# One ring of three PSUM banks for turned probabilities and jobs, in place of one bank and two

## What is computed

```python
qkv = (x @ w_qkv).reshape(b, s, NUM_HEADS + 2 * NUM_KV, HEAD_DIM)
...
logits = jnp.einsum('bkpsd,bktd->bkpst', q, k) * scale
attn = jax.nn.softmax(logits.astype(jnp.float32), axis=-1)
combined = jnp.einsum('bkpst,bktd->bkpsd', attn, v.astype(jnp.float32)).astype(v.dtype)
...
return combined @ w_out
```

## Time and profile before

| | us |
|---|---|
| median of 3 runs | 3746.49 |
| lowest, highest | 3746.47, 3748.72 |
| the profiled execution | 3749.1 |
| its span, first to last instruction | 3747.4 |
| TensorE busy | 3391.4 |
| VectorE busy | 2742.9 |
| ScalarE busy | 2060.3 |
| GpSimd busy | 1140.2 |

### The profile page before, as it was taken

How to read it: one execution, slowest core, us unless ns; L and a number is a source line. 1 busy time by engine, 2 the same in 40 slices (tenths; PEclk the granted TensorE clock), 3 DMA queues, 4 the chain that set the end, 5 groups by cost and what they waited for, 6 DMA issues and landing times.

```text
span 3747.4 us, 52800 instructions
## 1 busy us (share of the span) xinstructions
PE 3391.4 (90%) x19398; PEld 2853.6 (76%) x19398; DVE 2742.9 (73%) x5009; ACT 2060.3 (55%) x3891; POOL 1140.2 (30%) x1507
## 2 busy tenths in 40 slices
PE   2788888879999999999999999999999999999993
PEld 1677777767878888788887887878887888788872
DVE  4787897757786777776777677776777767776764
ACT  2567766745545555555555555555555555556541
POOL 2577877842212212122121221212212121122103
PEclk9999999989999999999999999999999999999996
DMA  2000001110000000000000001000000010000000
GB/s 75 20 24 24 25 28 35 43 32 12 15 14 27 21 13 12 12 21 26 12 13 13 23 19 40 12 12 24 26 14 13 18 29 25 12 23 22 25 6 28
DMA packets 81103, 83.27 MB, mean 22 GB/s; under 512 B 8272, under 2 KB 76496, under 8 KB 80720
## 3 DMA queue, kind: packets, MB, share of 16 engines
q1 hardware_dynamic: 80848, 79.89, 7.2%
HBM read 74.62 MB, written 5.24 MB: 21 GB/s over the span
## 4 chain that ended last, share of the span: by engine, by line
PE 64%; DVE 8%; ACT 5%; issue 1%; DMA 0%; POOL 0%; DVEq 0%; SPq 0%; ACTq 0%; POOLq 0%
PE at_ps_t L1717 12%; PE at_ps_job L35 6%; PE at_ps_job L37 6%; PE at_ps_job L36 6%; PE at_ps_o L37 5%; PE at_ps_o L35 5%; PE at_ps_o L36 5%; PE at_ps_s L37 5%; PE at_ps_s L35 5%; PE at_ps_s L36 5%; DVE at_probT_lo L1598 2%; ACT at_probT_hi L1544 1%; ACT x_resident L1587 1%; PE at_ps_job L852 1%; DVE ch_r L742 1%
## 5 line engine op out<-in xcount | busy, mean ns | idle before, releaser
L1544 ACT ACTIVATE at_probT_hi<-at_ps_t 128x512 fp32r<-128x512 f32 x1024 | 611.2, 597 | 1152.4 <-PE at_ps_t L1717 1152.2
L1598 DVE TENSOR_TENSOR at_probT_lo<-at_ps_t,at_probT_hi 128x512 fp32r<-128x512 f32 x1024 | 705.1, 689 | 377.1 <-ACT at_probT_hi L1544 365.4
L1717 PE MATMUL at_ps_t<-ident,x_resident 128*128 128x128 f32 x4096 | 625.6, 275 | 103.1 <-DVE at_probT_lo L1598 92.3
L1717 PEld LDWEIGHTS at_ps_t<-ident,x_resident 128*128 128x128 f32 x4096 | 481.0, 140 | 254.9 <-DVE at_probT_lo L1598 113.8
L1652 DVE TENSOR_REDUCE at_neg_max<-at_ps_s 128x1 f32<-128x1024 f32 x512 | 623.0, 1217 | 10.9 <-PE at_ps_s L37 2.4
L1587 ACT ACTIVATE x_resident<-at_ps_s,at_neg_max 128x1024 f32<-128x1024 f32 x512 | 569.4, 1112 | 12.9 <-DVE at_neg_max L1652 9.8
L1527 POOL TENSOR_TENSOR at_w_hi<-at_w_raw,ch_cols 128x256 fp32r<-128x256 f32 x192 | 117.7, 613 | 1196.5 <-PE at_ps_job L37 1175.4
L35 PE MATMUL at_ps_o<-at_probT_hi,at_v_lo 128*128 128x512 f32 x1024 | 445.8, 435 | 2.4 <-DVE at_oT_lo L1628 2.4
L35 PE MATMUL at_ps_s<-at_k_hi,at_q_lo 128*128 128x512 f32 x1024 | 447.3, 437 | 0.0
L37 PE MATMUL at_ps_s<-at_k_lo,at_q_hi 128*128 128x512 f32 x1024 | 405.3, 396 | 0.0
L37 PE MATMUL at_ps_o<-at_probT_lo,at_v_hi 128*128 128x512 f32 x1024 | 404.0, 395 | 0.0
(11 more groups left out here) (275 smaller groups left out, 7781.5 us busy)
## 6 DMA issues: line engine op xcount, KB each, us to landing
at_w_raw<-attn_w SPq DMA_DIRECT2D x256, 128.0 KB, 2.3
at_w_raw<-mlp_w SPq DMA_DIRECT2D x112, 128.0 KB, 2.3
li_wq_raw<-lin_q_w SPq DMA_DIRECT2D x64, 128.5 KB, 2.1
li_wo_raw<-lin_out_w SPq DMA_DIRECT2D x32, 256.0 KB, 3.0
x_resident<-x SPq DMA_DIRECT2D x4, 1024.0 KB, 10.8
out<-x_resident SPq DMA_DIRECT2D x4, 1024.0 KB, 5.0
li_raw<-mlp_w SPq DMA_DIRECT2D x16, 128.0 KB, 2.4
ch_r<-lin_kv_w SPq DMA_DIRECT2D x1, 1024.0 KB, 6.7
```

The lines of the kernel that those rows point to most:

```text
L1544: nc.scalar.activation(ph[:, i // TC, 4 * half:4 * half + 4, (i % TC) * P:(i % TC + 1) * P], ps_t[:], ACT.Copy).then_inc(s_ph, 1)
L1598: nc.vector.tensor_tensor(pl[at], ps_t[:], ph[at].bitcast(F32), ALU.subtract).then_inc(s_pl, 1)
L1717: last = nc.tensor.transpose(ps_t[:, j, :], prob[:, i % 2, kt * P:(kt + 1) * P], sh.ident[:])
```

## The change

The two sets of banks become one ring of three. `Plan` numbers the two turns of a slot and its jobs together, in TensorE's order but with both turns first (`claim`), and before a turn or job is issued `wait_emptied` waits for whoever reads out the claim three back. `at_ps_t` is gone; turns are written to and read from `at_ps_job`, which has three banks. Both turns' waits for the turn before them go. The order of instructions on every engine is the same as before; what changes is the bank that an instruction names and the semaphore count it waits for. The linear attention phase uses the same classes with two banks and no turns, as before.

```diff
-    def __init__(self, begin, end, rows, chain, tail):
+    def __init__(self, begin, end, rows, chain, tail, banks, turns=lambda t: ()):
...
         for t in range(self.begin, self.end):
+            for number in turns(t):
+                self.claim["TURNED", number] = len(self.taker)
+                self.taker.append(("turn", number + 1))
             for kind, v, part in rows(t):
                 self.count(kind, v, part)
...
         self.place[key] = len(self.place)
+        self.claim[key] = len(self.taker)
...
-        self.taker.append((kind in ACT_TAKES, counts[key]))
+        self.taker.append(("act" if kind in ACT_TAKES else "dve", counts[key]))
...
     def bank(self, kind, v, part):
-        return self.ps_job[self.plan.place[kind, v, part] % 2]
+        return self.ps_job[self.plan.claim[kind, v, part] % self.plan.banks]
+
+    def turned_bank(self, number):
+        return self.ps_job[self.plan.claim["TURNED", number] % self.plan.banks].rearrange("p (j t) -> p j t", j=4)
...
+def wait_emptied(pe, c, n):
+
+
+    if n >= c.plan.banks:
+        by, count = c.plan.taker[n - c.plan.banks]
+        pe.wait_ge({"act": c.took, "dve": c.taken, "turn": c.turned_low}[by], count)
+
+
 def claim(pe, c, kind, v, part):
-
-
-    n = c.plan.place[kind, v, part]
-    if n >= 2:
-        by_act, count = c.plan.taker[n - 2]
-        pe.wait_ge(c.took if by_act else c.taken, count)
-    return c.ps_job[n % 2]
+    wait_emptied(pe, c, c.plan.claim[kind, v, part])
+    return c.bank(kind, v, part)
...
+def turned_tile(t):
+
+
+    u, slot = divmod(t, TB)
+    back, i = (u - 1, slot + TB - 2) if slot < 2 else (u, slot - 2)
+    return (back, i) if 0 <= back < UNITS else None
+
+
+def turns_at(t):
+    if turned_tile(t):
+        u, i = turned_tile(t)
+        yield 2 * TB * u + 2 * i
+        yield 2 * TB * u + 2 * i + 1
...
         ps_s = [ctx.enter_context(nc.psum_tensor(f"at_ps_s{i}", [P, S], F32)) for i in range(2)]
-        ps_t = ctx.enter_context(nc.psum_tensor("at_ps_t", [P, 4, P], F32))
         ps_o = ctx.enter_context(nc.psum_tensor("at_ps_o", [P, CH], F32))
-        ps_job = [ctx.enter_context(nc.psum_tensor(f"at_ps_job{i}", [P, CH], F32)) for i in range(2)]
+        ps_job = [ctx.enter_context(nc.psum_tensor(f"at_ps_job{i}", [P, CH], F32)) for i in range(3)]
...
             def turn(u, i, half):
+                number = 2 * TB * u + 2 * i + half
+                wait_emptied(pe, c, plan.claim["TURNED", number])
+                turned = c.turned_bank(number)
                 for j in range(4):
                     kt = 4 * half + j
-                    last = nc.tensor.transpose(ps_t[:, j, :], prob[:, i % 2, kt * P:(kt + 1) * P], sh.ident[:])
+                    last = nc.tensor.transpose(turned[:, j, :], prob[:, i % 2, kt * P:(kt + 1) * P], sh.ident[:])
                 last.then_inc(s_pT, 1)
...
                 if turned:
+                    back, i = turned
                     pe.wait_ge(s_exp, TB * back + i + 1)
-                    if 2 * TB * back + 2 * i:
-                        pe.wait_ge(s_pl, 2 * TB * back + 2 * i)
                     turn(back, i, 0)
...
                 values_part(u, slot, 0)
                 if turned:
-                    pe.wait_ge(s_pl, 2 * TB * back + 2 * i + 1)
                     turn(back, i, 1)
```

More of the change, by code:

```diff
@@ L352 @@
 class Plan:
-    def __init__(self, begin, end, rows, chain, tail):
-        self.rows = rows
+    def __init__(self, begin, end, rows, chain, tail, banks, turns=lambda t: ()):
+        self.rows, self.banks = rows, banks
         self.at, self.first, self.last = {}, {}, {}
@@ L378, in __init__ @@
                 self.no[kb] = i if kinds != ("X",) else kb[1]
-        self.place, self.high, self.by_dve, self.by_act, self.taker = {}, {}, {}, {}, []
+        self.place, self.claim, self.high, self.by_dve, self.by_act, self.taker = {}, {}, {}, {}, {}, []
         for t in range(self.begin, self.end):
+            for number in turns(t):
+                self.claim["TURNED", number] = len(self.taker)
+                self.taker.append(("turn", number + 1))
             for kind, v, part in rows(t):
@@ L474, in sem @@
             return sh.sem(f"{tag}_{name}")
-        self.plan, self.ps_job, self.tile = plan, ps_job, tile
+        self.plan, self.ps_job, self.tile, self.turned_low = plan, ps_job, tile, None
         self.ln = Ln(sh, tag)
@@ L921, in linear_attention_phase @@
     plan = Plan(BEGIN, END + LAG + 2, lambda t: rows.get(t, []),
-                [("QA", 2, 0), ("QA", 3, 0), ("QB", 0, LOOP + LAG + 2), ("FA", 0, 0), ("X", 0, 3 * LOOP + 1)], [])
+                [("QA", 2, 0), ("QA", 3, 0), ("QB", 0, LOOP + LAG + 2), ("FA", 0, 0), ("X", 0, 3 * LOOP + 1)], [], 2)
     made, high, by_dve = plan.made, plan.high, plan.by_dve
@@ L1387, in attention_phase @@
                 [("QB", 1, 4), ("FA", 1, 0), ("X", 1, 0), ("QB", 2, 0), ("FA", 2, 0), ("X", 2, 0), ("FB", 0, TB * H + TB),
-                 ("QB", 3, 0), ("FA", 3, 0), ("X", 3, 0), ("FB", 1, 2 * TB * H + TB), ("FB", 2, 3 * TB * H + TB)], [("FB", 3)])
+                 ("QB", 3, 0), ("FA", 3, 0), ("X", 3, 0), ("FB", 1, 2 * TB * H + TB), ("FB", 2, 3 * TB * H + TB)], [("FB", 3)], 3, turns_at)
     made, high, by_dve, by_act = plan.made, plan.high, plan.by_dve, plan.by_act
@@ L1433, in attention_phase @@
         c.first_x = 1
+        c.turned_low = s_pl
         block = ctx.enter_context(nc.Block())
@@ L1544, in probT_high @@
                 nc.scalar.activation(ph[:, i // TC, 4 * half:4 * half + 4, (i % TC) * P:(i % TC + 1) * P],
-                                     ps_t[:], ACT.Copy).then_inc(s_ph, 1)
+                                     c.turned_bank(2 * TB * u + 2 * i + half), ACT.Copy).then_inc(s_ph, 1)
             def job_high(u, slot, late=False):
@@ L1573, in _ @@
                 has_last, has_own = u >= 1, u < UNITS
-                back, i = (u - 1, slot + TB - 2) if slot < 2 else (u, slot - 2)
-                turned = has_last if slot < 2 else has_own
+                turned = turned_tile(t)
                 if turned:
+                    back, i = turned
                     probT_high(back, i, 0)
@@ L1597, in probT_low @@
                 at = (slice(None), i // TC, slice(4 * half, 4 * half + 4), slice((i % TC) * P, (i % TC + 1) * P))
-                nc.vector.tensor_tensor(pl[at], ps_t[:], ph[at].bitcast(F32), ALU.subtract).then_inc(s_pl, 1)
+                nc.vector.tensor_tensor(pl[at], c.turned_bank(2 * TB * u + 2 * i + half), ph[at].bitcast(F32),
+                                        ALU.subtract).then_inc(s_pl, 1)
             def job_low(u, slot, late=False):
```

## The result

The changed kernel takes 3615.5 us (median of 4 runs, 3613.0 to 3617.2), the one before 3747.6 beside it (4 runs): a ratio of 0.9646, 95% interval 0.9634 to 0.9657, or 132 us less. The forecast was 113 us less, in a range that holds the result. Of the 136, 4.1 lie ahead of the first turn (823.9 us before, 819.8 after), where the two kernels run the same work; attention itself is 131 shorter.

The account below looks back on a forecast made before the run. TensorE, busy 90% of the span, was taken to set the pace, with turn waits its main idle time. Of 155 us lost, 42 stay, so 113 are gained: 3746.5 - 113 = 3633.5 us, own range 3606 to 3665, wider 3594 to 3680.

Parts of the forecast that it names:

- The loss of 155 us: All halts at turns in attention: 103.1 us idle plus 272 x 0.2, about 155 us, between 103 and 166.
- Kinds two and three: Turn 0 late after a lone output projection (0.26 us lost) or without a job (1.20 instead of 0.23); both vanish.
- Late V: V evictions done one slot late make Y jobs wait for their bank; 94 such jobs, 3 us in all.
- The room before the output's bank: Between the output's low part and the next at_ps_o product: 0.80 us; of 2.1 us there, 1.3 stays gained.
- The share that stays lost: Part of the 155 us not gained: 42 us, from compares 26, statistics and layernorm 10, GELU 6.
- Compares: Router compare windows beside attention, six blocks: 50 us lost in all, half likely to stay lost, 26.
- GELU: Six GELU windows: 23 us lost in all; ScalarE late by its tables, a quarter stays, 6.
- 1 (TensorE runs ahead freely, 3591.5): TensorE in attention gains the whole 155 us, nothing coming back as other waits: 3591.5 us; chance 0.14.
- 2 (every loaded slot bound by VectorE): VectorE or ScalarE bounds every loaded slot, and waits only change their name: 3683.5 us; chance 0.12.
- 3: Turn 0's halts are TensorE's own cost at a change of operands, little is gained: 3746 us; chance 0.02.
- 4 (late jobs): Late V jobs block later ring claims and the scores behind; 3769 us if 2.1 us later each; chance 0.02.
- 5 (clock): Granted clock falls to 0.94 over the steady 2,400 us, adding some 144 us: 3778 us; chance 0.02.

Follow-up runs that it names:

- e3: Changed kernel with both old turn waits put back, so only the sharing of banks is left; 3743.3 us, ratio 0.9984 to the kernel before.
- e4: Changed kernel with the router's compares on 8 columns, so the ranks are not computed; 3596.8 us, ratio 0.9595 to the kernel before.
- e8: Changed kernel with a plain copy in place of GELU and its bias; 3601.8 us, ratio 0.9614 to the kernel before.
- e6: Changed kernel with ScalarE making the output's high part ahead of the exponential in slots 1 and 5; 3604.4 us, ratio 0.9613 to the kernel before.

## Why the prediction was right, and where its terms were off

**The loss of 155 us.** Right. The starts give back 146 at the turns, and some 5 are still lost before turn 0 in the changed kernel. The price of a halt, idle time plus 0.2 us, is borne out by the same: 98 us of idle time went for those 146.

**Kinds two and three.** Right, and a third of the whole: by the starts, 90 turns behind a lone Y job lost 27 us and 28 turns behind a slot without a job 27; in the changed kernel they lose none. There turn 0 starts 0.12 us after a lone Y job (0.38 before) and 0.23 after the last product of a slot without a job (1.20 before):

```profile
1964.17 0.28 PE L37 MATMUL at_ps_job<-at_w_lo,at_oT_hi 128*128 128x256 f32 x1
1964.29 0.60 PE L1746 MATMUL at_ps_job<-ident,x_resident 128*128 128x128 f32 x4
...
1967.72 0.39 PE L37 MATMUL at_ps_o<-at_probT_lo,at_v_hi 128*128 128x512 f32 x1
1967.95 0.60 PE L1746 MATMUL at_ps_job<-ident,x_resident 128*128 128x128 f32 x4
```

In e3, with the banks shared and the waits back, the two distances are 0.33 and 1.16 us: at most 0.05 of each came from the sharing.

**Late V.** Right in kind and size. The forecast had 3 us. Of the 1.7 us of waits for `at_v_lo`, 0.7 stand before Y jobs and 1.0 before a K or Q job at the start of attention (834.46 us); by the starts, Y jobs lose 2.8.

**The room before the output's bank.** The walk through one place came out close. The place in the changed kernel, TensorE and then VectorE and ScalarE:

```profile
1956.30 0.40 PE L37 MATMUL at_ps_s<-at_k_lo,at_q_hi 128*128 128x512 f32 x1
1957.28 0.47 PE L35 MATMUL at_ps_o<-at_probT_hi,at_v_lo 128*128 128x512 f32 x1 [0.58 <-DVE at_oT_lo L1654]
...
1956.44 0.69 DVE L1654 TENSOR_TENSOR at_oT_lo<-at_ps_o,at_oT_hi 128x512 fp32r<-128x512 f32 x1 [1.16 <-ACT at_oT_hi L1588]
```

```profile
1949.21 1.11 ACT L1612 ACTIVATE x_resident<-at_ps_s,at_neg_max 128x1024 f32<-128x1024 f32 x1 [0.86 <-DVE at_neg_max L1678]
...
1954.72 1.12 ACT L1612 ACTIVATE x_resident<-at_ps_s,at_neg_max 128x1024 f32<-128x1024 f32 x1 [1.31 <-DVE at_neg_max L1678]
```

The product starts 0.98 us after the matmul before it, 0.75 late; I had 0.8. The exponentials lie 5.51 us apart; I had 5.7. Against the matmul of 2008.40 this product comes 1.3 us sooner than before, as forecast. The sum of that walk was loose, though: with the output's low part at 2018.7 it gives a wait of 0.7, and the 0.6 us by which that part comes sooner had only 0.40 behind it; the trace has 0.66.

**The share that stays lost: the terms that were mis-sized.** The forecast let 42 us stay (its own halves make 41, since half of 50 is 25 and not 26), and about 23 did. Its range, 3606 to 3665, is not what its bounds of 78 and 155 us give, 3591.5 to 3668.5, and the text does not say why; the result lies in both. The waits before `at_ps_o` that it named as a sign, 15 to 30 us, were 7.3 as idle time and 11.0 by the starts, and under half of these lie beside compares (4.5, e4). By stretch, six blocks each, measured by the starts of the same matmuls in both traces:
- Compares: "half is likely to stay lost: 26", a gain of 24. Measured 41. The failed step is that I took one place and made half of the whole stretch of it. That place stands behind two halts in a row. Seven turns get 0.3 us or more back in each of the six stretches, and the ring's waits before `at_ps_o` there are one of 0.76 and one of 0.27 us in three of them and one of 0.3 in the others. e4 gives what the compares still cost with the ring, 4.5 us and not 26.
- Statistics and layernorm: a gain of 40. In the six routed windows it is 26 (4.5 in the one shown), of 31 lost, about as forecast.
- GELU: a quarter was to stay, 6, a gain of 17. Measured 12: in three blocks 1.5, as in the window shown, in the others 2.5. With the 8.3 us that e8 finds left there, four tenths stay. Here the forecast erred the other way. ScalarE loads its table twice a step, and in the ring two different claims stand behind it:

```profile
2080.12 1.28 ACT L639 ACT_TABLE_LOAD   x1
...
2083.78 1.28 ACT L1612 ACT_TABLE_LOAD   x1
```

```profile
2089.95 0.39 PE L35 MATMUL at_ps_job<-at_w_hi,at_oT_lo 128*128 128x256 f32 x1 [0.23 <-DVE at_v_lo L1649]
2091.77 0.63 PE L1746 MATMUL at_ps_job<-ident,x_resident 128*128 128x128 f32 x4 [0.40 <-DVE at_probT_lo L1623]
```

The Y job at 2089.95 waits for a late V, and turn 0 at 2091.77 for the turn before it, which is the case with two jobs between. This second wait stands in all six blocks, the first in three. e8 takes the table loads away, and both are gone.

The forecast's gain was 24 for the compares, 17 for GELU and 40 + 32 = 72 for all else; measured are 41, 12 and 132 - 53 = 79. Errors of +17, -5 and +7 make the 19 us by which the sum was off.

**The rivals.** 1 (TensorE runs ahead freely, 3591.5): refuted as put, since 15 us of new waits came, 11.0 before `at_ps_o` and 4.3 at jobs, but it was nearer than I thought: the time is 24 us above it and 18 below the forecast. e6 takes the largest of these waits away. 2 (every loaded slot bound by VectorE): refuted, by waits before `at_ps_o` of 7.3 us and not above 60, and by e4. 3: refuted, e3. 4 (late jobs): 1.7 us. 5 (clock): the granted clock from 1000 to 3400 us stayed 1.00, with TensorE's idle time down from 13 us in 400 to 1.5. The Trainium skill's section on psum-queue depth-cycling ("TensorE: Matmul & The Clock Gate") describes a kernel whose clock went up and down from small idle gaps while it cycled through PSUM banks. This case's trace does not agree: three banks cycle here, and the granted clock stays at 1.00 from 1000 to 3400 us.

**What stays open.** Why turn 0 behind a lone Y job starts 0.05 us sooner in e3 than in the kernel before; and what makes a turn's read-out late where no compare stands beside it, since no run shortens that chain.

## What to carry over

Where two kinds of tile take turns on one engine and each has its own small set of banks, pool the banks: a ring in order of issue gives each claim the whole time of a slot, and the sharing costs nothing if what is read late is not claimed soon. Price a halted TensorE by the distance of starts or, somewhat high, by the idle time of its weight loads (156 us here where the starts give 146); the idle time before the matmul itself was a third too small. Where two kernels issue the same instructions in the same order, compare the starts one by one and over all blocks, since one window times six gave 9 us for GELU where the six together gave 12. After such a wait is gone, walk to the next one: the edit of e6 was worth nothing before and 13 us after, and it cost only a place in ScalarE's queue where that engine stood idle.

## What was not expected of the hardware

A halted TensorE loses more than its idle time shows: 98 us of idle time before turns went, the starts came 146 us closer, and the time fell by 132. And two waits on one queue are not independent: taken away alone they gave 61 and 34 us, together 132.
